# A circulant filter matrix from frequencies sorted by parity, and the latents' weights in two wider products

## The chip, the cores and the metric

The kernel runs on one core of one Trainium2 chip. The time is the device time of one execution in microseconds (us). Three runs of the kernel before gave a median of 418.75 us.

## The reference, cut to what matters

```python
D = _fractal_dimension(x)                 # from the first 1024 normalised values
filt = _wave_filter(D, E)                 # E = 256 complex factors, a function of |frequency|
x1 = ifft(fft(x, axis=-1) * filt, axis=-1).real
lat = x1 @ W_el + b_el                    # W_el: 256 x 24
bits = (sigmoid(lat) > 0.5)
corrected = _golay_correct(bits)
attn = x1 + corrected @ W_le + b_le
...
xn = _layernorm(x)
x = x + attn(xn) + ffn(xn)                # ffn: 256 -> 1024, exact gelu, -> 256, with biases
```

x has 2 x 4096 tokens of 256 float32 numbers. The filter depends only on the absolute frequency, so filtering is the product with a symmetric circulant matrix C of 256x256 whose first row c is a sum of cosines (and, by the way it is laid out here, of sines) with the filter as weights.

## The kernel before, in words

**Tiles.** The tokens are worked on in 16 chunks of 512, with the 256 features on two blocks of 128 partitions. In each chunk TensorE computes the hidden layer (`up`, L882, eight blocks m of 128 hidden units), its product with w2 (`down`, L900 and L905), the latents (`latents`, L926), the filter (`filtered`, L937), the code checks (`checks`, L950) and the correction's product (`le_products`, L956). Precision is kept with pairs: each float32 number is split into a "hi" part (rounded to the format float32r, which TensorE takes in one pass) and a "lo" part (the rest). ScalarE makes the gelu and the hi parts, VectorE the lo parts, the normalisation and the sums. GpSimd takes square roots and `uv`, the sums and differences of the two feature halves (`turn`).

**Sums and differences.** With u = first half + second half and v = first half - second half, the circulant falls apart into two 128x128 matrices, one for u and one for v. They are kept in `c_f` as two halves of 128 columns, and split into `c_hi` and `c_lo`. The latents' weights are the matrix's product with W_el, turned the same way.

**The work around the change** is in chunk 0, and is done once:
- SyncE's queue loads `basis` (L298) behind the weights; behind it stand `xt(1)`, `codes` and `latent`.
- VectorE makes `wel_t` from W_el (L817 to L819), then `bias` and `le_t` (L822, L823), for which ScalarE waits (L516).
- GpSimd computes `filt_w`, the 256 filter weights, two on each partition.
- ScalarE scales `basis` with them into `basis_w` (L526).
- TensorE makes the matrix in `p_l` (`circulant`, L1025), after `down(0, 4)`.
- ScalarE copies it to `c_f` and `c_hi` (L531, L532).
- TensorE multiplies `c_f` with `wel_t` in `p_g` (`latent_weights`, L1034 and L1035), after `down(0, 6)`.
- ScalarE casts that to `cw` (L536), waiting for `cw_made`; VectorE adds the low part (L837).
- Only then ScalarE makes the hi part of chunk 1's normalised columns (`columns_hi(1, 1)`, L411), and VectorE the lo part (`columns_lo`, L601), for which `up(1, 1, 0)` waits.

All orders are written out by hand: each engine runs its own list, and waits on semaphores. The products of `circulant` and `latent_weights` have plain float32 operands; in the trace each of them is two TensorE instructions of the same shape, with a weight load each. VectorE's list from the end of chunk 0 on:

```python
            scale(1, 1)
            hidden_lo(0, 7)
            ...
            columns_lo(1, 1)
            turned_lo(0)
            ...
            first_branch_chunk(1, 1)
```

and `first_branch_chunk` begins with the statistics (L569), `add_ffn` (L635), `hidden_lo(c, 0)` (L611), `aggregate` (L574) and `take_bits(b, ...)` (L616), for whose `word` TensorE waits before its second `latents`.

Of the kernel before, what the change touches and what calls it, by code (L numbers as in the profile page):

```python
# [7 lines left out]
F32, F32R, BF16, U32 = mybir.dt.float32, mybir.dt.float32r, mybir.dt.bfloat16, mybir.dt.uint32  # L8
ALU = mybir.AluOpType
# [3 lines left out]
P = 128  # L13
TOKENS, E, HID, LAT, SYN = 2 * 4096, 256, 1024, 24, 12
# [4 lines left out]
KB = E // P  # L19
MB = HID // P  # L20
HF = E // 2
# [12 lines left out]
SEG = 32  # L34
# [34 lines left out]
def build(nc, x, xt, small, latent, w1, w2, ident, consts, basis, codes, out):  # L69
    ctx = ExitStack()  # L70
    with ctx:
        def sb(name, shape, dt):
            return ctx.enter_context(nc.sbuf_tensor(name, shape, dt))

        def ps(name, shape, dt):
            return ctx.enter_context(nc.psum_tensor(name, shape, dt))

        def sem(name):
            return ctx.enter_context(nc.semaphore(name))
# [30 lines left out]
        con = sb("con", [P, K_END], F32)  # L110
        code_f = sb("code_f", [P, 2, P], F32)
        code = sb("code", [P, 2, P], BF16)
        bias = sb("bias", [P, KB], F32)
        wel_t = sb("wel_t", [P, 3, LAT], F32)
        basis_sb = sb("basis_sb", [P, KB, HF + E], F32)
        basis_w = sb("basis_w", [P, KB, E], F32)
        c_f = sb("c_f", [P, 2, HF], F32)
        c_hi = sb("c_hi", [P, 2, HF], F32R)
        c_lo = sb("c_lo", [P, 2, HF], F32R)
# [27 lines left out]
        filt_w = sb("filt_w", [P, KB], F32)  # L147
# [15 lines left out]
        p_l = ps("p_l", [P, BANK], F32)  # L163
        p_g = ps("p_g", [P, BANK], F32)
# [18 lines left out]
        basis_wd, c_made, c_copied, c_hi_ready = sem("basis_wd"), sem("c_made"), sem("c_copied"), sem("c_hi_ready")  # L183
        wel_turned, cw_made, cw_hi_ready, c_ready = sem("wel_turned"), sem("cw_made"), sem("cw_hi_ready"), sem("c_ready")
# [9 lines left out]
        turned, u_hi, u_lo = sem("turned"), sem("u_hi"), sem("u_lo")  # L194
# [22 lines left out]
        def half_tokens(part, g):  # L217

            return part[:, :, g * GTOK:(g + 1) * GTOK]

        def half_bank(g):

            return p_s[:, g, :].rearrange("p (k t) -> p k t", k=KB)
# [179 lines left out]
        def _(act):  # L403
# [23 lines left out]
            def gelu(c, m, first=False):  # L427

                act.wait_ge(up_done, MB * c + m + 1)
                if not (first and m < 2):  # L430

                    act.wait_ge(h_lo_done, MB * c + m - 1)
                nc.scalar.activation(h[m % 2][:], p_h[:, m % 2, :], ACT.Gelu,  # L433
                                     bias=small_sb[:, S_B1 + m:S_B1 + m + 1]).then_inc(gelu_done, 1)
# [74 lines left out]
            for g in range(2):  # L509
                last = nc.scalar.copy(half_tokens(xc0, g), half_bank(g))  # L510
# [12 lines left out]
            act.wait_ge(basis_in, 16)  # L523
            act.wait_ge(filt_made, 1)
            for k in range(KB):
                nc.scalar.mul(basis_w[:, k, :], basis_sb[:, k, HF:HF + E], filt_w[:, k:k + 1]).then_inc(basis_wd, 1)  # L526
            gelu(0, 7, first=True)
            hidden_hi(0, 7, first=True)
            act.wait_ge(c_made, 1)
# [22 lines left out]
        def _(dve):  # L552
# [6 lines left out]
            def then(ins):  # L559

                links[0] += 1
                ins.then_inc(link, 1)
                dve.wait_ge(link, links[0])
# [186 lines left out]
            for j in range(HALF):  # L750
                dve.wait_ge(x_first[j], 16)
                last = nc.vector.bn_stats(stats[:, j, :], x_sb[0][:, j, :])
# [4 lines left out]
            for j in range(HALF, CT):  # L757
                last = nc.vector.bn_stats(stats[:, j, :], x_sb[0][:, j, :])
# [55 lines left out]
            hidden_lo(0, 4)  # L814
            dve.wait_ge(small_in, 16)
            wel = small_sb[:, S_WEL:S_END].rearrange("p (k l) -> p k l", k=KB)
            nc.vector.tensor_tensor(wel_t[:, 0, :], wel[:, 0, :], wel[:, 1, :], ALU.add)  # L817
            nc.vector.tensor_tensor(wel_t[:, 1, :], wel[:, 0, :], wel[:, 1, :], ALU.subtract)
            nc.vector.tensor_tensor(wel_t[:, 2, :], wel[:, 1, :], wel[:, 0, :], ALU.subtract).then_inc(wel_turned, 1)  # L819
            then(nc.vector.tensor_tensor(bias[:], small_sb[:, S_BLE:S_BLE + KB], small_sb[:, S_B2:S_B2 + KB], ALU.add))  # L820
            dve.wait_ge(latent_in, 16)
            nc.vector.tensor_tensor(le_t[:, 0, :], latent_sb[:, 1:1 + HF], latent_sb[:, 1 + HF:1 + E], ALU.add)  # L822
# [31 lines left out]
        def _(pe):  # L854
            mm = nc.tensor.matmul
# [164 lines left out]

            def circulant():

                pe.wait_ge(basis_wd, KB)
                for k in range(KB):
                    last = mm(p_l[:, 0:E], basis_sb[:, k, 0:HF], basis_w[:, k, :], start=(k == 0), stop=(k == KB - 1))  # L1025
                last.then_inc(c_made, 1)

            def latent_weights():

                pe.wait_ge(c_copied, 1)  # L1030
                pe.wait_ge(wel_turned, 1)
                for k in range(KB):
                    at = SEG + k * LAT
                    mm(p_g[:, at:at + LAT], c_f[:, 0, :], wel_t[:, 0, :], start=True, stop=False, skip_group_check=True)  # L1034
                    last = mm(p_g[:, at:at + LAT], c_f[:, 1, :], wel_t[:, 1 + k, :], start=False, stop=True,  # L1035
                              skip_group_check=True)
                last.then_inc(cw_made, 1)

            def summed_over(at, n, parts, ready, done):
# [10 lines left out]
            for g in range(2):  # L1050

                pe.wait_ge(xn0_done, g + 1)
                for k in range(KB):
                    for j in range(HALF):
                        last = nc.tensor.transpose(half_bank(g)[:, k, j * P:(j + 1) * P],
                                                   xn0[:, g * HALF + j, k * P:(k + 1) * P], id_sb[:])
# [28 lines left out]
def constants():  # L1085

    import numpy as np

    f4 = np.float32
    con = np.zeros((P, K_END), f4)  # L1090
    lx = np.log(np.array(SCALES, np.float64))
    n = len(SCALES)
    den = n * np.sum(lx * lx) - np.sum(lx) ** 2

    coef = -(n * lx - np.sum(lx)) / den


    at = np.arange(FRE)
    row, half = 2 * (at // (2 * KB)) + at % 2, at // 2 % KB
    number = (E * row + P * half + np.arange(P)[:, None] + 1).reshape(P, 1, FRE)  # L1100
    con[:, K_MASK:K_MASK + NS * FRE] = (number <= np.array(PREFIX)[:, None]).reshape(P, NS * FRE)
    con[:, K_CLOG:K_CLOG + NS * FRE] = (np.log(number) * coef[:, None]).reshape(P, NS * FRE)
    con[:, K_NUM:K_NUM + FRE] = number[:, 0]
    con[:, K_INVN:K_INVN + NS] = [1.0 / n for n in PREFIX]

    r = np.arange(E)
    freq = np.where(r <= E // 2, r, r - E // 2)
    ang = 2.0 * np.pi * ((freq[:, None] * r[None, :]) % E) / E
    basis = np.where((r <= E // 2)[:, None], np.cos(ang), np.sin(ang)).astype(f4)
    ka = (freq / E).astype(f4) + f4(1e-8)  # L1110
    weight = np.where((r == 0) | (r == E // 2), 1.0, 2.0) / E / 2
    turned = np.concatenate([basis[:, :HF], basis[:, :HF] + basis[:, HF:], basis[:, :HF] - basis[:, HF:]], axis=1)
    by_block = lambda v: v.reshape(KB, P).T

    ka = ka.astype(np.float64)
    con[:, K_C1:K_C1 + KB] = by_block(np.pi - ka)
    con[:, K_C1 + KB:K_C1 + COLS] = by_block(np.pi / 2 + ka)
    con[:, K_C2:K_C2 + KB] = by_block(1.0 + 0.5 * ka)
    con[:, K_C2 + KB:K_C2 + COLS] = by_block(1.0 + 0.1 * ka * ka)
    con[:, K_ODD:K_ODD + PAIRS * COLS] = np.repeat(SINE[1::2], COLS)  # L1120
    con[:, K_EVEN:K_EVEN + PAIRS * COLS] = np.repeat(SINE[0::2], COLS)
    con[:, K_WK:K_WK + KB] = by_block(weight)
    con[:, K_WK + KB:K_WK + COLS] = 1.0
    a = np.array([[1, 1, 1, 0, 1, 1, 1, 0, 0, 0, 1, 1], [1, 1, 0, 1, 1, 1, 0, 0, 0, 1, 1, 0],
# [4 lines left out]
                  [1, 0, 0, 1, 1, 0, 0, 1, 1, 0, 0, 1], [0, 1, 1, 0, 0, 1, 1, 0, 0, 1, 1, 0]], np.int64)  # L1129
    rows = np.concatenate([a.T, np.eye(SYN, dtype=np.int64)], axis=1)  # L1130

    codes = np.zeros((P, 2, P), f4)
    fixed = np.zeros((P, GROUPS, SEG), f4)
    for par in range(2):
        here, before = SEG * par, SEG * (1 - par)
        codes[here:here + LAT, par, ROWS:ROWS + SYN] = rows.T
        fixed[:] = 0.0
        fixed[before:before + LAT, :, 0:LAT] = 25.0 * np.eye(LAT)[:, None, :]  # L1140
        fixed[2 * SEG, :, 0:LAT] = 9.5
        fixed[ROWS:ROWS + SYN, :, 0:SYN] = (1.0 - 13.0 * np.eye(SYN))[:, None, :]
        codes[:, par, 0:ROWS] = fixed.reshape(P, ROWS)
    return np.eye(P, dtype=f4), con, turned.astype(f4), codes.reshape(P, 2 * P)


def layouts(inputs):
# [37 lines left out]
```

## Time and profile before

| | us |
|---|---|
| median of three runs (lowest, highest) | 418.75 (418.73, 419.31) |
| the profiled execution, its own time | 418.89 |
| its span, first to last instruction | 417.1 |
| TensorE busy | 409.1 (98%) |
| VectorE busy | 307.3 (74%) |
| ScalarE busy | 218.7 (52%) |
| GpSimd busy | 73.7 (18%) |

How to read it: the profile shows one execution. PE is TensorE's products, PEld its weight loads (which overlap the products), DVE VectorE, ACT ScalarE, POOL GpSimd, SP SyncE. L1025 is line 1025 of the kernel before. The ends of products are modelled, so starts are safer than durations, and a stretch in which each product begins before the last has ended counts as busy. In rows of instructions the numbers are start, duration, engine, line, operation, output, inputs and their sizes; "x2" says that two neighbours were merged, and then the duration runs from the first one's start to the last one's end. A square bracket holds the engine's idle time before the row, and what ended it. The clock that TensorE was granted is 1.00 of full speed in all stretches shown.

### The profile page before, as it was taken

Reading aid. Unit: us, or ns where it says so; the run is one execution under the profiler, and the core shown is the slowest. Engines: PE = TensorE matmul, PEld = TensorE weight load, DVE = VectorE, ACT = ScalarE, POOL = GpSimd, SP = SyncE. Lnnn points to the kernel's source line nnn. Section 1 sums busy time; section 2 is a strip of 40 time slices with the busy share of each in tenths; the row PEclk is TensorE's granted clock in tenths of the full one; section 3 lists DMA queues with packets and bytes.
Section 4 is the critical chain, followed back from the end, with each engine's and each line's share of the span. In section 5 each row is a group of like instructions: output and inputs, shape, how many; then the busy total and the mean of one; then the engine's idle time right before and its main releaser. Section 6 shows DMA issues by size and latency. Waiting matters only on the chain.

```text
span 417.1 us, 5569 instructions
## 1 busy us (share of the span) xinstructions
PE 409.1 (98%) x1789; PEld 325.8 (78%) x1789; DVE 307.3 (74%) x503; ACT 218.7 (52%) x325; POOL 73.7 (18%) x102
## 2 busy tenths in 40 slices
PE   8998999999999999999999999999999999999996
PEld 4786787887888788787887878788787878878774
DVE  7888696968669686776867778686786868676654
ACT  3957446555365554536555464554536655464641
POOL 2161321212012121111212012121111212012000
PEclk9999999999999999999999999999999999999999
DMA  7562223133331123332122332223333111111011
GB/s 221 200 210 95 101 61 92 52 101 103 101 101 56 51 95 101 101 101 72 53 76 101 101 101 90 26 86 101 101 101 98 53 51 51 51 51 50 2 50 50
DMA packets 16495, 36.04 MB, mean 86 GB/s; under 512 B 5452, under 2 KB 8164, under 8 KB 16484
## 3 DMA queue, kind: packets, MB, share of 16 engines
q1 hardware_dynamic: 16340, 35.78, 27.2%
q10 hardware_dynamic: 144, 0.13, 0.1%
q8 instruction: 5, 0.08, 0.1%
q14 instruction: 6, 0.05, 0.1%
HBM read 27.45 MB, written 8.45 MB: 86 GB/s over the span
## 4 chain that ended last, share of the span: by engine, by line
PE 93%; DVE 4%; DMA 1%; issue 1%; ACT 0%; POOL 0%; SPq 0%; DVEq 0%
PE p_h L882 41%; PE p_f L900 27%; PE p_f L905 13%; PE p_s L937 5%; PE p_l L926 3%; PE p_s L956 2%; PE p_g L950 1%; DMA x_sb<-x 1%; DVE stats L569 1%; DVE xt_sb L644 0%; DVE xt_sb L650 0%; DVE xT_lo L601 0%; DVE w_lo L732 0%; DVE h_lo L611 0%; DVE xt_sb L726 0%
## 5 line engine op out<-in xcount | busy, mean ns | idle before, releaser
L433 ACT ACTIVATE h<-p_h,small_sb 128x512 f32<-128x512 f32 x128 | 88.1, 688 | 155.1 <-PE p_h L882 155.0
L611 DVE TENSOR_TENSOR h_lo<-h,h_hi 128x512 fp32r<-128x512 f32 x128 | 90.1, 704 | 71.4 <-ACT h_hi L441 71.2
L900 PE MATMUL p_f<-h_hi,w_hi 128*128 128x512 f32 x254 | 99.7, 392 | 0.0
L900 PE MATMUL p_f<-h_hi,w_lo 128*128 128x512 f32 x254 | 99.0, 390 | 0.0
L882 PE MATMUL p_h<-xT_hi,w_hi 128*128 128x512 f32 (+1 forms) x258 | 86.1, 415 | 1.5 <-DVE xT_lo L601 1.0
L441 ACT CAST h_hi<-h 128x512 fp32r<-128x512 f32 x128 | 79.4, 620 | 5.8
L882 PE MATMUL p_h<-xT_lo,w_hi 128*128 128x512 f32 (+1 forms) x258 | 79.6, 390 | 0.1
L882 PE MATMUL p_h<-xT_hi,w_lo 128*128 128x512 f32 (+1 forms) x258 | 79.5, 389 | 0.0
L905 PE MATMUL p_f<-h_lo,w_hi 128*128 128x512 f32 x254 | 78.2, 389 | 0.0
L363 POOL TENSOR_TENSOR uv<-xn 128x512 f32<-128x512 f32 x30 | 43.6, 1475 | 127.7 <-DVE xn L596 127.7
L882 PEld LDWEIGHTS p_h<-xT_hi,w_hi 128*128 128x128 f32 x258 | 48.3, 189 | 11.9 <-DVE xT_lo L601 1.5
L882 PEld LDWEIGHTS p_h<-xT_lo,w_hi 128*128 128x128 f32 x258 | 48.3, 188 | 10.8 <-DVE xT_lo L767 0.3
L882 PEld LDWEIGHTS p_h<-xT_hi,w_lo 128*128 128x128 f32 x258 | 48.3, 188 | 10.7
L900 PEld LDWEIGHTS p_f<-h_hi,w_hi 128*128 128x128 f32 x254 | 47.7, 188 | 10.3
L905 PEld LDWEIGHTS p_f<-h_lo,w_hi 128*128 128x128 f32 x254 | 47.7, 188 | 10.1
L900 PEld LDWEIGHTS p_f<-h_hi,w_lo 128*128 128x128 f32 x254 | 47.7, 188 | 10.0
L346 POOL TENSOR_TENSOR var_eps<-mv,eps 128x4 f32<-128x4 f32 (+1 forms) x17 | 3.9, 227 | 173.3 <-DVE mv L574 173.3
L601 DVE TENSOR_TENSOR xT_lo<-xn,xT_hi 128x1024 fp32r<-128x1024 f32 x15 | 32.7, 2179 | 0.8 <-ACT xT_hi L411 0.7
L635 DVE SCALAR_TENSOR_TENSOR xt_sb<-p_f,bias,xt_sb 128x512 f32 (+1 forms) x30 | 21.1, 746 | 12.5 <-PE p_f L905 12.5
L606 DVE TENSOR_TENSOR uv_lo<-uv,uv_hi 128x1024 fp32r<-128x1024 f32 x16 | 19.6, 1226 | 9.2 <-ACT uv_hi L418 9.2
L411 ACT CAST xT_hi<-xn 128x1024 fp32r<-128x1024 f32 x15 | 15.8, 1054 | 13.5 <-DVE xn L596 13.5
L591 DVE TENSOR_TENSOR xn<-xt_sb,rows_sb 128x1024 f32<-128x1024 f32 x15 | 18.3, 1223 | 5.9 <-DMA rows_sb<-rows_dram 5.5
(117 smaller groups left out, 331.4 us busy)
## 6 DMA issues: line engine op xcount, KB each, us to landing
xt_sb<-xt SPq DMA_DIRECT2D x16, 512.0 KB, 5.2
x_sb<-x SPq DMA_DIRECT2D x15, 512.0 KB, 4.5
rows_sb<-rows_dram SPq DMA_DIRECT2D x15, 512.0 KB, 4.1
out<-xt_sb SPq DMA_DIRECT2D x15, 512.0 KB, 2.9
xt_sb<-w SPq DMA_DIRECT2D x3, 512.0 KB, 7.3
xt_sb<-w SPq DMA_DIRECT2D x2, 256.0 KB, 4.1
basis_sb<-basis SPq DMA_DIRECT2D x1, 384.0 KB, 8.8
x_sb<-x SPq DMA_DIRECT2D x2, 128.0 KB, 2.1
```

The costliest lines, as they stand in the source:

```text
L363: nc.gpsimd.tensor_tensor(uv[:, k, :], columns[:, 0, :], columns[:, 1, :], op).then_inc(turned, 1)
L433: nc.scalar.activation(h[m % 2][:], p_h[:, m % 2, :], ACT.Gelu, bias=small_sb[:, S_B1 + m:S_B1 + m + 1]).then_inc(gelu_done, 1)
L441: nc.scalar.copy(h_hi[m % HR][:], h[m % 2][:]).then_inc(h_hi_done, 1)
L591: nc.vector.tensor_tensor(xn[:, :, :], columns(c), to_halves(rows_sb[par][:, 0, :]), ALU.subtract).then_inc(centred, 1)
L601: nc.vector.tensor_tensor(xT_lo[par][:, :, :], xn[:, :, :], xT_hi[par][:, :, :].bitcast(F32), ALU.subtract).then_inc(t_lo, 1)
L606: nc.vector.tensor_tensor(uv_lo[:, :, :], uv[:, :, :], uv_hi[:, :, :].bitcast(F32), ALU.subtract).then_inc(u_lo, 1)
L611: nc.vector.tensor_tensor(h_lo[m % HR][:], h[m % 2][:], h_hi[m % HR][:].bitcast(F32), ALU.subtract).then_inc(h_lo_done, 1)
L635: nc.vector.scalar_tensor_tensor(out=xc, in0=p_f[:, k, :], scalar=bias[:, k:k + 1], in1=xc, op0=ALU.add, op1=ALU.add).then_inc(ffn_added, 1)
L882: last = mm(p_h[:, m % 2, tok], w[:, k, m * P:(m + 1) * P], xp[par][:, k, tok], start=(n == 0), stop=(n == 3 * KB - 1))
L900: mm(p_f[:, a, :], w[:, m, a * HF:(a + 1) * HF], h_hi[r][:], start=(m == 0 and w is w2_hi), stop=False, skip_group_check=True)
L905: last = mm(p_f[:, a, :], w2_hi[:, m, a * HF:(a + 1) * HF], h_lo[r][:], start=False, stop=(m == MB - 1), skip_group_check=True)
L937: last = mm(p_s[:, k, :], w[:, k, :], xp[:, k, :], start=(n == 0), stop=False, skip_group_check=True)
```

## The change

The 256 frequencies are sorted: the even ones come first and make the first block of 128 rows of `basis`, the odd ones the second. A cosine or sine of an even frequency has the same value 128 columns on, one of an odd frequency the opposite value. So the matrix for the sums needs the even block alone, and the matrix for the differences the odd block alone. `circulant` was two accumulating products of 256 columns and is now two separate products of 128 columns; each waits only for its own half of `basis_w`. `basis` shrinks from 128x2x384 to 128x2x128 numbers, `basis_w` from 256 to 128 columns per block, and the weights of the frequencies are doubled on the host. `wel_t` is laid out for both feature halves side by side, so that `latent_weights` is two accumulating products of 48 columns instead of four of 24; the sum part is written twice, with a broadcast operand.

```diff
--- before.py
+++ after.py
@@ -111,9 +111,9 @@
         code_f = sb("code_f", [P, 2, P], F32)
         code = sb("code", [P, 2, P], BF16)
         bias = sb("bias", [P, KB], F32)
-        wel_t = sb("wel_t", [P, 3, LAT], F32)
-        basis_sb = sb("basis_sb", [P, KB, HF + E], F32)
-        basis_w = sb("basis_w", [P, KB, E], F32)
+        wel_t = sb("wel_t", [P, 2, KB, LAT], F32)
+        basis_sb = sb("basis_sb", [P, KB, HF], F32)
+        basis_w = sb("basis_w", [P, KB, HF], F32)
         c_f = sb("c_f", [P, 2, HF], F32)
         c_hi = sb("c_hi", [P, 2, HF], F32R)
         c_lo = sb("c_lo", [P, 2, HF], F32R)
@@ -523,7 +523,7 @@
             act.wait_ge(basis_in, 16)
             act.wait_ge(filt_made, 1)
             for k in range(KB):
-                nc.scalar.mul(basis_w[:, k, :], basis_sb[:, k, HF:HF + E], filt_w[:, k:k + 1]).then_inc(basis_wd, 1)
+                nc.scalar.mul(basis_w[:, k, :], basis_sb[:, k, :], filt_w[:, k:k + 1]).then_inc(basis_wd, 1)
             gelu(0, 7, first=True)
             hidden_hi(0, 7, first=True)
             act.wait_ge(c_made, 1)
@@ -814,9 +814,11 @@
             hidden_lo(0, 4)
             dve.wait_ge(small_in, 16)
             wel = small_sb[:, S_WEL:S_END].rearrange("p (k l) -> p k l", k=KB)
-            nc.vector.tensor_tensor(wel_t[:, 0, :], wel[:, 0, :], wel[:, 1, :], ALU.add)
-            nc.vector.tensor_tensor(wel_t[:, 1, :], wel[:, 0, :], wel[:, 1, :], ALU.subtract)
-            nc.vector.tensor_tensor(wel_t[:, 2, :], wel[:, 1, :], wel[:, 0, :], ALU.subtract).then_inc(wel_turned, 1)
+            other = wel[:, 1, :].unsqueeze(1).broadcast_to([P, KB, LAT])
+            nc.vector.tensor_tensor(wel_t[:, 0, :, :], wel[:, 0, :].unsqueeze(1).broadcast_to([P, KB, LAT]), other, ALU.add)
+            for k in range(KB):
+                last = nc.vector.tensor_tensor(wel_t[:, 1, k, :], wel[:, k, :], wel[:, 1 - k, :], ALU.subtract)
+            last.then_inc(wel_turned, 1)
             then(nc.vector.tensor_tensor(bias[:], small_sb[:, S_BLE:S_BLE + KB], small_sb[:, S_B2:S_B2 + KB], ALU.add))
             dve.wait_ge(latent_in, 16)
             nc.vector.tensor_tensor(le_t[:, 0, :], latent_sb[:, 1:1 + HF], latent_sb[:, 1 + HF:1 + E], ALU.add)
@@ -1020,20 +1022,20 @@
 
             def circulant():
 
-                pe.wait_ge(basis_wd, KB)
+
                 for k in range(KB):
-                    last = mm(p_l[:, 0:E], basis_sb[:, k, 0:HF], basis_w[:, k, :], start=(k == 0), stop=(k == KB - 1))
+                    pe.wait_ge(basis_wd, k + 1)
+                    last = mm(p_l[:, k * HF:(k + 1) * HF], basis_sb[:, k, :], basis_w[:, k, :], start=True, stop=True,
+                              skip_group_check=True)
                 last.then_inc(c_made, 1)
 
             def latent_weights():
 
                 pe.wait_ge(c_copied, 1)
                 pe.wait_ge(wel_turned, 1)
-                for k in range(KB):
-                    at = SEG + k * LAT
-                    mm(p_g[:, at:at + LAT], c_f[:, 0, :], wel_t[:, 0, :], start=True, stop=False, skip_group_check=True)
-                    last = mm(p_g[:, at:at + LAT], c_f[:, 1, :], wel_t[:, 1 + k, :], start=False, stop=True,
-                              skip_group_check=True)
+                for a in range(2):
+                    last = mm(p_g[:, SEG:SEG + KB * LAT], c_f[:, a, :], wel_t[:, a, :, :].rearrange("p k l -> p (k l)"),
+                              start=(a == 0), stop=(a == 1), skip_group_check=True)
                 last.then_inc(cw_made, 1)
 
             def summed_over(at, n, parts, ready, done):
@@ -1105,11 +1107,13 @@
 
     r = np.arange(E)
     freq = np.where(r <= E // 2, r, r - E // 2)
-    ang = 2.0 * np.pi * ((freq[:, None] * r[None, :]) % E) / E
+
+    r = np.argsort(freq % 2, kind="stable")
+    freq = freq[r]
+    ang = 2.0 * np.pi * ((freq[:, None] * np.arange(HF)[None, :]) % E) / E
     basis = np.where((r <= E // 2)[:, None], np.cos(ang), np.sin(ang)).astype(f4)
     ka = (freq / E).astype(f4) + f4(1e-8)
-    weight = np.where((r == 0) | (r == E // 2), 1.0, 2.0) / E / 2
-    turned = np.concatenate([basis[:, :HF], basis[:, :HF] + basis[:, HF:], basis[:, :HF] - basis[:, HF:]], axis=1)
+    weight = np.where((r == 0) | (r == E // 2), 1.0, 2.0) / E
     by_block = lambda v: v.reshape(KB, P).T
 
     ka = ka.astype(np.float64)
@@ -1141,7 +1145,7 @@
         fixed[2 * SEG, :, 0:LAT] = 9.5
         fixed[ROWS:ROWS + SYN, :, 0:SYN] = (1.0 - 13.0 * np.eye(SYN))[:, None, :]
         codes[:, par, 0:ROWS] = fixed.reshape(P, ROWS)
-    return np.eye(P, dtype=f4), con, turned.astype(f4), codes.reshape(P, 2 * P)
+    return np.eye(P, dtype=f4), con, basis, codes.reshape(P, 2 * P)
 
 
 def layouts(inputs):
```

## Rows read from the trace of the kernel before

**Rows 1.** The page, parts 1 and 4: TensorE's busy time, and the chain's shares by engine

```profile
PE 409.1 (98%) x1789; PEld 325.8 (78%) x1789; DVE 307.3 (74%) x503; ACT 218.7 (52%) x325; POOL 73.7 (18%) x102
...
PE 93%; DVE 4%; DMA 1%; issue 1%; ACT 0%; POOL 0%; SPq 0%; DVEq 0%
```

**Rows 2.** Windows, a later chunk: stretch, length, busy us (count) by engine, clock

```profile
59.89:84.80 24.91, 24.91 (x110) 20.05 (x110) 18.54 (x30) 13.06 (x19) 4.25 (x5) 1.00 0.35 105
```

**Rows 3.** Waits of TensorE, whole span: total us, times, longest (two of five)

```profile
PE p_h L882 <- DVE xT_lo L601: 1.0, 1, 1.0
...
PE p_l L926 <- DVE word L616: 0.5, 1, 0.5
```

**Rows 4.** Timeline, the first products of chunk 1

```profile
34.98 0.73 PE L882 MATMUL p_h<-xT_hi,w_hi 128*128 128x512 f32 x2 [1.02 <-DVE xT_lo L601]
```

**Rows 5.** The chain that ended last, 28 to 35 us: start, us, what

```profile
28.03 0.86 PE p_l L1025 x4
...
32.25 0.24 PE p_g L1035 x2
...
32.52 0.20 ACT cw L536
32.71 0.96 ACT xT_hi L411
...
33.70 1.23 DVE xT_lo L601
```

**Rows 6.** Timeline of VectorE

```profile
17.51 0.20 DVE L799 TENSOR_TENSOR fr_b<-con,fr_s 128x40 f32<-128x40 f32 x1
...
22.16 0.18 DVE L817 TENSOR_TENSOR wel_t<-small_sb 128x24 f32<-128x24 f32 x1
...
24.86 3.47 DVE L611 TENSOR_TENSOR h_lo<-h,h_hi 128x512 fp32r<-128x512 f32 x2 [1.70 <-ACT h_hi L441]
...
29.82 1.23 DVE L596 TENSOR_TENSOR xn<-xn,rows_sb 128x1024 f32<-128x1024 f32 x1
...
36.09 0.42 DVE L842 TENSOR_TENSOR le<-le_r,le_mid 24x256 bf16<-24x256 f32 x1
36.54 1.40 DVE L569 BATCH_NORM_STATS2 stats<-x_sb 128x6 f32<-128x256 f32 x4
```

**Rows 7.** Timeline of ScalarE in the second half of chunk 0

```profile
23.18 0.42 ACT L516 ACTIVATE le<-le_t 24x256 bf16<-24x256 f32 x1 [2.53 <-DVE le_t L823]
...
26.28 0.91 ACT L526 ACTIVATE basis_w<-basis_sb,filt_w 128x256 f32<-128x256 f32 x2
...
28.93 0.38 ACT L531 COPY c_f<-p_l 128x256 f32<-128x256 f32 x1 [0.52 <-PE p_l L1025]
...
32.52 0.20 ACT L536 CAST cw<-p_g 128x48 fp32r<-128x48 f32 x1 [2.93 <-PE p_g L1035]
```

**Rows 8.** Timeline of weight loads around the latents' products

```profile
31.62 0.30 PEld L1035 LDWEIGHTS p_g<-wel_t,c_f 128*128 128x128 f32 x2
...
32.29 0.19 PEld L900 LDWEIGHTS p_f<-h_hi,w_hi 128*128 128x128 f32 x1
```

**Rows 9.** Timeline of weight loads, 256-column products of the first chunk

```profile
9.12 0.31 PEld L882 LDWEIGHTS p_h<-xT_hi,w_hi 128*128 128x128 f32 x2
9.35 0.31 PEld L882 LDWEIGHTS p_h<-xT_hi,w_lo 128*128 128x128 f32 x2
```

**Rows 10.** Lines L1042 and L1035: duration ns least/median/most, starts, forms

```profile
L1042 PE MATMUL p_g<-fr_d,ones x2: 166/208/250, 19.4 to 19.5; 128*128 128x1 f32 x2
...
L1035 PE MATMUL p_g<-wel_t,c_f x4: 269/269/269, 31.6 to 32.2; 128*128 128x24 f32 x4
```

**Rows 11.** Timeline of SyncE: the issue of the load of basis

```profile
6.76 0.75 SPq L298 DMA_DIRECT2D basis_sb<-basis  x1
```

**Rows 12.** DMA issues: count, KB each, median us from issue to landing

```profile
basis_sb<-basis SPq DMA_DIRECT2D x1, 384.0 KB, 8.8
...
code_f<-codes SPq DMA_DIRECT2D x1, 128.0 KB, 9.0
```

## The prediction

> **What bounds the kernel now.** I read the page first. TensorE is busy for 409.1 of the 417.1 us, and the chain that ended last is TensorE for 93% [rows 1]. So there are two ways to gain: fewer TensorE instructions, or less of the time in which TensorE stands still. Next come the stretches of the trace. Each later chunk takes 24.91 us and TensorE is busy in all of it, with the granted clock at 1.00, which is the 2.4 GHz level, throughout [rows 2]. The waits of TensorE over the whole span are five, and the last two are those that matter here: 1.0 us for `xT_lo` and 0.5 us for `word` [rows 3]. Both lie between 34 and 41 us, behind the code that is changed, and none of the five lies after 42 us. So what is gained before chunk 1 starts is kept to the end, if chunk 1 really starts earlier.
>
> **Where the changed code lies.** It runs once, in chunk 0. `up(1, 1, 0)` starts at 34.98, and TensorE stood still for 1.02 us before it, from 33.96 [rows 4]. The chain shows why: the latents' products (L1034, L1035) until 32.49, ScalarE's cast of `cw` (L536), its cast `xT_hi` (L411), VectorE's `xT_lo` (L601), then TensorE [rows 5]. ScalarE works in order, so `columns_hi(1, 1)` stands behind the wait for `cw_made`, although its input `xn` was ready at 31.05 (L596 starts at 29.82 and takes 1.23) [rows 6]. ScalarE stood idle 2.93 us before L536 [rows 7]. After `xT_lo`, VectorE works without a gap (L606, L842, L569, L635, L611, L574, L616) until `word` (L569 starts 0.03 after L842 ended [rows 6]), and TensorE's second wait ends there [rows 3]. Both waits of TensorE therefore hang on the same event, the end of L1035, and move with it. This makes the changed products a critical stage, even though TensorE has an idle microsecond right behind them: shortening only other TensorE work behind `cw_made` would give nothing.
>
> **Products of the filter matrix.** Before, four instructions (two for each float32 product) of 256 columns follow each other; the chain has them from 28.03 and gives them 0.86 us, 0.215 each [rows 5]. After, there are again four, each with 128 columns. Half the streaming of 0.215 is 0.108. The weight load sets another floor. Near it are the loads of the 24-column products, which are so short that only loads pace them: from the second pair of loads to the first load behind the last pair, three pairs, it is 32.29 - 31.62 = 0.67 us, some 0.1125 per instruction [rows 8]. A row with about this amount of streaming is the 256-column single-pass product of the first chunk, whose pairs of loads are 0.23 apart, 0.115 each [rows 9]. I take 0.115: 4 x 0.115 = 0.46, a gain of 0.86 - 0.46 = 0.40 us. The bounds are 0 (the instructions keep the 0.215 of now) and 0.43 (pure streaming, 0.86 / 2). This gain reaches the latents' products, since TensorE works without a gap from one to the other and nothing it needs is late: `c_f` is copied at 29.31 [rows 7] and is wanted shortly before 31.62 [rows 8], or 0.40 earlier then; `h_lo` of m = 6 is ready when L611's pair ends at 28.33 [rows 6] and is wanted after 31.0.
>
> **The waits on `basis_wd`.** Before, one wait for both scaled halves, after, one for each. The two scalings end at 27.19 (26.28 + 0.91) [rows 7] and the chain comes to the products at 28.03 [rows 5], so neither wait binds: nothing. ScalarE's scalings shrink from 128x256 to 128x128. Halved at best, the stage of 0.91 falls to between 0.45 and 0.91. What is behind it, `gelu(0, 7)` and `hidden_hi(0, 7)`, is over 0.52 before ScalarE is released by `c_made` [rows 7]; the gain there is hidden, and since `c_made` comes only 0.40 earlier, no queue forms.
>
> **The latents' weights.** Four products of 24 columns become two of 48, eight instructions become four. A pair costs 0.67 / 3 = 0.223 between starts, so two pairs fewer are 0.45 us [rows 8]. The wider ones should take no more between starts, since even 128 streamed columns come to 0.108, under the pace of the loads. Their own duration grows, though: the longer of the two kinds is 250 ns at 1 column and 269 at 24, that is 19 ns for 23 columns [rows 10], so 24 more columns make the last one end 0.02 later. The gain is 0.43 us, with bounds of 0.40 (if the added columns were paid in all four) and 0.45.
>
> **VectorE.** The three `wel_t` operations of 128x24 take about 0.18 each [rows 6]. After, they are one of 128x48 with broadcast inputs and two of 128x24. The nearest row with a broadcast operand is L799, 128x40 in 0.20 [rows 6]. So 0.02 us more, between 0 and 0.05. They hold up `le_t`, for which ScalarE waits (2.53 us before L516 [rows 7]), and so `gelu(0, 5)` and then the whole gapless VectorE chain from L611 up to `xn`. But that chain delivers `xn` at 31.05, and ScalarE will want it at about 32.71 - 0.83 = 31.88, so 0.02 disappears in a cover of 0.8 us. With that cover gone it would cost its 0.02.
>
> **The transfer of `basis`** shrinks from 384 to 256 KB, in rows of 512 instead of 1536 bytes. It is issued at 6.76 [rows 11] and landed 8.8 us later [rows 12], at 15.6, and is wanted by L526 at 26.28 [rows 7]. Behind it in the queue are `xt(1)`, `codes` and `latent`; codes land 9.0 us after their issue [rows 12], some 17.5, and ScalarE wants them after L516, so after 23.18 [rows 7]. Either way nothing, with 5 us of cover.
>
> **Sum.** 0.40 + 0.43 = 0.83 us on the end of L1035. `xT_lo` then starts at 33.70 - 0.83 = 32.87 [rows 5]. TensorE finishes `down(0, 7)` at 33.96 - 0.83 = 33.13 and waits again, to 34.15. The profiled execution took 418.89 us, 1.79 more than its span (a constant part); less 0.83 that is 418.06. It lies 0.14 above the median of 418.75, so for the median I predict 418.75 - 0.83 = 417.92 us, a ratio of 0.9980.
>
> **A rule beside it.** The rows have the short instructions at 0.1125 to 0.115 each [rows 8, 9]. The Trainium skill, "TensorE: Matmul & The Clock Gate", section "Back-to-back issue gap", gives about 81 ns for each pair of load and product with 128 columns in a sustained stream, and "LDWEIGHTS (loading the stationary operand)" gives columns / 1.2, which is 107 ns for 128. By the 81 ns the filter matrix would gain 0.86 - 0.32 = 0.54 and the latents' weights only 4 x 0.081 - 0.02 = 0.30, together 0.84; the result would hardly differ. The rows speak for the load's 107 ns as the floor.
>
> **Rivals.**
> (A) The filter products keep their pace of 0.215, because float32 instructions are paced by something other than columns. For it: no float32 product of 128 columns that is not a transpose is in the trace. Against it: the 24-column ones run at 0.1125. Only 0.43 would be left: 418.32.
> (B) Another wait takes the place of `cw_made`, for instance VectorE in chunk 1 standing for something that doesn't move. `x(2)` is such a thing, but VectorE began L569 0.03 after L842 ended [rows 6], so there is no sign that it waited; `xn` would allow a move of up to 0.8 or more. Then nothing would be gained: 418.75.
> (C) Short instructions run quicker than the rows let me think (0.081 in the filter products, 0.1125 kept for the removed ones): 0.54 + 0.43 = 0.97: 417.78.
> (D) Slower. The broadcast `wel_t` operation is slow, as an input with a repeated stride might be. The VectorE chain from L611 at 24.86 to `xn` [rows 6] starts from ScalarE's wait for `le_t`. Delays up to about 0.83 + 0.83 = 1.7 us are covered or repaid by the gain; it decides from there, ten times the 0.18 of such an operation now. At 2.7 us it would be 419.75. Against it: L799 with its broadcast takes 0.20 [rows 6].
>
> **How the numbers follow.** What a measurement of this kernel can tell from no change is about 0.2%, 0.84 us; my forecast of 0.83 lies on that edge. Chances: the forecast, a gain of 0.75 to 0.90, 0.74; A 0.08; B 0.06; C 0.07; D and other losses 0.05. The forecast's case is split nearly in two by the edge, 0.36 above and 0.38 below. Faster: 0.36 + 0.07 = 0.43, and 0.02 for mixed cases, 0.45. Within: 0.38 + 0.08 + 0.06 less those 0.02, 0.50. Slower: 0.05. The likeliest case's own range is 417.85 to 418.0; the three runs shown scatter by 0.02 below and 0.56 above the median. The range that leaves out B and D and takes in A and C is 417.7 to 418.4.
>
> **What would show it.** Right: L1025's four instructions take about 0.46 us in the chain; the latents' products begin near 31.1 and are four; L536 starts near 31.69, L601 near 32.87, `up(1, 1, 0)` near 34.15; TensorE's waits are still 1.0 and 0.5 us; chunk 2 starts 0.83 earlier and every chunk still takes 24.91. Wrong: a start of L536 that moved by less than 0.75 (A), a start of chunk 2 that moved less than L536 did (B), `wel_t` operations above 0.3 us (D), or a new wait in the later chunks.

## The result, and the profile after

The changed kernel takes 415.85 us (median of 6 runs, 415.69 to 416.11), the kernel before in the same series 418.95: a ratio of 0.9927, 95% interval 0.9917 to 0.9936. That is 3.1 us less, where 0.83 were predicted, and it lies outside the range. The profiled execution's span fell from 417.1 to 414.1 us.

First the part that was predicted. The chain that ended last, of the kernel after, 28 to 35 us (start, us, what):

```profile
28.03 0.45 PE p_l L1028 x4
28.48 0.92 PE p_f L902 x4
...
31.21 0.39 PE p_g L1037 x4
...
31.63 0.20 ACT cw L536
31.83 0.96 ACT xT_hi L411
...
32.81 1.23 DVE xT_lo L601
```

Against [rows 5]: the filter products took 0.86 us and take 0.45, for the same four instructions. The latents' products took 0.82 (31.67 to 32.49) and take 0.39. The cast of `cw` moved from 32.52 to 31.63, `xT_lo` from 33.70 to 32.81. The timeline of TensorE at the start of chunk 1, after:

```profile
34.09 0.73 PE L884 MATMUL p_h<-xT_hi,w_hi 128*128 128x512 f32 x2 [1.04 <-DVE xT_lo L601]
```

It was at 34.98 [rows 4]: 0.89 us earlier, 0.83 was predicted. The waits of TensorE, after:

```profile
PE p_h L884 <- DVE xT_lo L601: 1.0, 1, 1.0
...
PE p_l L928 <- DVE word L616: 0.6, 1, 0.6
```

To within 0.1 us they are what they were [rows 3], and no new one stands behind them. So where are the other 2.1 us? Look at the chunks that the change doesn't touch. The chain of the kernel before, one later chunk (`latents`, `up`, `filtered`), and the start of the next chunk's `latents`:

```profile
88.42 0.93 PE p_l L926 x4
89.35 1.39 PE p_h L882 x6
90.74 1.40 PE p_s L937 x6
...
113.33 0.93 PE p_l L926 x4
```

The same of the kernel after:

```profile
87.35 0.91 PE p_l L928 x4
88.26 1.36 PE p_h L884 x6
89.62 1.36 PE p_s L939 x6
...
112.12 0.91 PE p_l L928 x4
```

From `latents` to `latents` it was 113.33 - 88.42 = 24.91 us and is 112.12 - 87.35 = 24.77. The products are the same in number, shape and order, there is no idle time in either, and the clock is 1.00 in both. Six products of 512 columns took 1.39 or 1.40 in this stretch, and now take 1.36. That is their pace in the rest of the chunk too, apart from a short stretch behind the 16-bit products of `checks` and `le_products`, which both kernels have (1.38). The start of TensorE's last product says it for the whole kernel. Before, then after:

```profile
412.59 0.39 PE L915 MATMUL p_f<-h_lo,w_hi 128*128 128x512 f32 x1
```

```profile
409.61 0.39 PE L917 MATMUL p_f<-h_lo,w_hi 128*128 128x512 f32 x1
```

From the start of chunk 1 it was 412.59 - 34.98 = 377.61 us and is 409.61 - 34.09 = 375.52, 2.09 less, which is 15 chunks by 0.14. With the 0.89 ahead of chunk 1 these are 2.98 of the span's 3.0 us.

### The profile page after: what moved, and what is told of

Same layout as the page of the kernel before. It is cut to its first block, busy times and chain, and to the rows that moved or that the text cites. A ratio compares the mean times of both kernels' runs of the same rounds, so it can differ in the third digit from the quotient of the medians.

```text
span 414.1 us, 5561 instructions
## 1 busy us (share of the span) xinstructions
PE 406.1 (98%) x1785; PEld 325.0 (78%) x1785; DVE 307.2 (74%) x503; ACT 218.7 (53%) x325; POOL 73.8 (18%) x102
## 4 chain that ended last, share of the span: by engine, by line
PE 93%; DVE 4%; DMA 1%; issue 1%; ACT 0%; POOL 0%; SPq 0%; DVEq 0%
PE p_h L884 41%; PE p_f L902 27%; PE p_f L907 14%; PE p_s L939 5%; PE p_l L928 3%; PE p_s L958 2%; PE p_g L952 1%; DMA x_sb<-x 1%; DVE stats L569 1%; DVE xt_sb L644 0%; DVE xt_sb L650 0%; DVE xT_lo L601 0%; DVE w_lo L732 0%; DVE h_lo L611 0%; DVE xt_sb L726 0%
```

## Experiments

**Where the tiles lie.** A product on TensorE has a stationary operand (the weights, loaded by an instruction of its own, PEld in the trace) and a moving one (the columns that are streamed past it). Both are tiles in SBUF, the on-chip memory. Tiles lie there in the order in which they are declared, each size rounded up to 32 bytes per partition. The change alters three sizes ahead of `c_f`, `c_hi`, `c_lo` and `cw`: `wel_t` 288 to 384 bytes, `basis_sb` 3072 to 1024, `basis_w` 2048 to 1024. So these four, and all tiles behind them, lie 2976 bytes lower. In the later chunks, `c_hi` and `c_lo` are the stationary operands of `filtered`, `cw` that of `latents`. The moving operands (`xT_hi`, `xT_lo`, `uv_hi`, `uv_lo`) and those of `up` and `down` are large tiles ahead of the altered ones and did not move.

**e1: the kernel before, with `wel_t` one slot larger.**

```diff
-        wel_t = sb("wel_t", [P, 3, LAT], F32)
+        wel_t = sb("wel_t", [P, 4, LAT], F32)
```

> The kernel before, with one line changed: wel_t is declared with 4 slots of 24 instead of 3, 384 bytes per partition instead of 288, and the fourth is not used. No instruction changes, but everything declared behind wel_t (basis_sb, basis_w, c_f, c_hi, c_lo, cw, idle, word, cor, le3 and others) moves by 96 bytes, so that the starts of these tiles, which are 32 past a multiple of 64 bytes in the kernel before, become multiples of 64, as in the changed kernel. Theory ALIGN (the 0.14 us that each later chunk gains come from where the tiles lie in SBUF): the chunks fall from 24.91 to 24.77 us, chunk 1 still starts at 34.98, and the time falls by 14 x 0.14 = 2.0 us, to about 416.8. Theory STREAM (they come from TensorE's program being shorter by four product and four load instructions, so that the loop's body lies elsewhere): nothing changes, 418.9. Theory HEAD (the later chunks gain because chunk 1 starts at another moment against the transfers): nothing changes, 418.9.

Measured: 417.01 us, ratio to before 0.9946 (0.9927 to 0.9966). The chain of e1:

```profile
88.29 0.91 PE p_l L926 x4
89.19 1.36 PE p_h L882 x6
90.55 1.36 PE p_s L937 x6
...
113.05 0.91 PE p_l L926 x4
```

113.05 - 88.29 = 24.76, and chunk 1 started at 35.04, as late as before. An unused fourth slot, without one instruction changed, brings the whole gain of the later chunks. STREAM and HEAD fall.

**e2: the changed kernel with a gap of 32 bytes.**

```diff
+        gap = sb("gap", [P, 8], F32)
         basis_sb = sb("basis_sb", [P, KB, HF], F32)
```

> The changed kernel with an unused tile of 32 bytes per partition declared ahead of basis_sb, so that the tiles behind it start 32 bytes past a multiple of 64 again, as in the kernel before. No instruction changes. ALIGN: chunks of 24.91 us again, and only the gain ahead of chunk 1 is left: 418.95 - 0.89 = 418.06 us. STREAM and HEAD: 415.85, as the changed kernel.

Measured: 417.52 us, ratio 0.9959 (0.9946 to 0.9972); chunks of 24.85, not the 24.91 that was expected. The place matters, but not as "a multiple of 64 or not".

**e3 and e4: which stationary operand.** Both are the kernel before with two gaps of 32 bytes.

```diff
 e3
+        gap = sb("gap", [P, 8], F32)
         cw = sb("cw", [P, KB, P], F32R)
+        gap2 = sb("gap2", [P, 8], F32)
         stats = sb("stats", [P, CT, 6], F32)
 e4
+        gap = sb("gap", [P, 8], F32)
         c_f = sb("c_f", [P, 2, HF], F32)
...
+        gap2 = sb("gap2", [P, 8], F32)
         cw = sb("cw", [P, KB, P], F32R)
```

> The kernel before with an unused tile of 32 bytes ahead of cw and another behind it: of the tiles behind wel_t, cw alone (the stationary operand of latents) starts at a multiple of 64 bytes, all others stay 32 past one. The slow stretch of the kernel before begins among the latents' products and runs on over the filter's products (c_hi, c_lo) and up(c, 2) and down(c, 0). ALIGN, if cw alone starts it and the filter's products inherit it: chunks of 24.77. ALIGN, if each misaligned stationary operand costs its own: between 24.77 and 24.91, nearer the upper end since six filter products stand against four of the latents. STREAM, HEAD, or tiles other than the stationary ones (word, cor, le3): 24.91.

> The counterpart: c_f, c_hi and c_lo start at multiples of 64 bytes, cw and everything behind it 32 past one. ALIGN, if cw alone starts the slow stretch: it is shorter, since the filter's products no longer feed it, or unchanged, 24.80 to 24.91. ALIGN, if the cost is the filter's: 24.77 to 24.80. STREAM, HEAD: 24.91.

Measured: e3 418.70 us and chunks of 24.88; e4 417.41 and 24.81 (one run each). In e3 only `cw` moved, and the later chunks gained 0.03; in e4 `c_hi` and `c_lo` moved too, and `filtered` takes 1.38 instead of 1.40 in the chain. So the place of each counts. How much of the 0.14 belongs to which these two don't say: as the table below shows, no operand reached in them the place where the cost is gone.

**e5 and e6: 64 bytes.** e6 is the changed kernel with a gap of 64 bytes ahead of `basis_sb`. e5 has two of 32, ahead of `id_sb` and ahead of `wel_t`.

```diff
 e5
+        gap = sb("gap", [P, 8], F32)
         id_sb = sb("id_sb", [P, P], F32)
...
+        gap2 = sb("gap2", [P, 8], F32)
         wel_t = sb("wel_t", [P, 2, KB, LAT], F32)
 e6
+        gap = sb("gap", [P, 16], F32)
         basis_sb = sb("basis_sb", [P, KB, HF], F32)
```

> The changed kernel with an unused tile of 32 bytes ahead of id_sb and another ahead of wel_t, so that id_sb, con, code_f and code also start at multiples of 64 bytes (they are 32 past one in both kernels), and wel_t and all behind it still do. In the changed kernel a slow stretch is left in every chunk, behind the check's product (L952), whose stationary operand is code. ALIGN: it shrinks or goes; it holds some 0.04 us of excess over the usual 0.227 per product, so 14 x 0.04 = up to 0.6 us less, 415.3 at best. If the stretch comes from the product being of 16-bit type and not from its place, nothing changes: 415.85.

> The changed kernel with an unused tile of 64 bytes ahead of basis_sb: all starts behind it are still multiples of 64, but no longer of 128. ALIGN with 64 bytes as the unit: chunks of 24.77 us, time 415.85. ALIGN with 128 or 256 bytes as the unit: chunks between 24.77 and 24.91.

Measured: e5 417.96 us (ratio 0.9972, 0.9962 to 0.9981), e6 418.01 (one run), with chunks of 24.90 and 24.89. ALIGN by 64 bytes falls: all the starts in question are multiples of 64 here, and the chunks are nearly as slow as before. The slow stretch behind the check's product didn't shrink in e5 either: the four products of `down` behind it still take 0.93.

**e7 and e8: the two parts of the change alone.** e7 is the kernel before with the new `wel_t` and the two wide products; e8 is the changed kernel with those undone.

```diff
 e7
-        wel_t = sb("wel_t", [P, 3, LAT], F32)
+        wel_t = sb("wel_t", [P, 2, KB, LAT], F32)
...
-                for k in range(KB):
-                    at = SEG + k * LAT
...
+                for a in range(2):
+                    last = mm(p_g[:, SEG:SEG + KB * LAT], c_f[:, a, :], wel_t[:, a, :, :].rearrange("p k l -> p (k l)"),
```

> The kernel before with the second part of the change alone: wel_t in the new layout of 384 bytes, and the latents' weights in two products of 48 columns. basis and the filter products stay. The new wel_t moves the tiles behind it by 96 bytes, as in e1. ALIGN: this part brings the whole gain of the later chunks, 2.0 us, and 0.45 of the gain ahead of chunk 1: about 416.5. STREAM or HEAD: 418.5.

> The changed kernel with the second part undone: wel_t in the old layout of 288 bytes and four products of 24 columns; the filter matrix from even and odd frequencies stays. The tiles behind wel_t start 32 past a multiple of 64 again. They lie a multiple of 1024 bytes below their place in the kernel before, where e2 had them 128 bytes elsewhere, and e2 lost 1.3 of the 2.1 us. ALIGN: the later chunks are slow again; if the place modulo 256 or more matters beside that modulo 64, 24.91 us each as before, and the time is 418.95 - 0.43 = 418.5; if only the place modulo 64 matters and e2's 24.85 belong to the changed program, 24.85 and 417.7. STREAM or HEAD: 24.77, 416.3.

Measured: e7 416.42 us (ratio 0.9934, 0.9919 to 0.9949), chunks of 24.77, chunk 1 at 34.50; e8 418.60 (ratio 0.9990, 0.9979 to 1.0001), chunks of 24.90. So the latents' part brings 0.66% of the 0.73% that both bring, most of it by the size of a tile. The filter part alone can't be told from no change, although its products take 0.45 us in its chain too. e8's tiles lie a multiple of 1024 bytes from their place before and cost the same as there, where e2's, 128 bytes from e8's, cost less.

**e9 to e12: which rule.** The gaps:

```diff
 e9   (the changed kernel)
+        gap = sb("gap", [P, 32], F32)
         basis_sb = sb("basis_sb", [P, KB, HF], F32)
 e10  (the changed kernel)
+        gap = sb("gap", [P, 8], F32)
         xt_sb = sb("xt_sb", [P, CHUNKS, KB, CTOK], F32)
 e11  (the changed kernel)
+        gap = sb("gap", [P, 40], F32)
         code = sb("code", [P, 2, P], BF16)
...
+        gap2 = sb("gap2", [P, 24], F32)
         wel_t = sb("wel_t", [P, 2, KB, LAT], F32)
...
+        gap3 = sb("gap3", [P, 32], F32)
         word = sb("word", [P, CTOK], BF16)
 e12  (the changed kernel)
+        gap = sb("gap", [P, 8], F32)
         xn = sb("xn", [P, KB, CTOK], F32)
...
+        gap2 = sb("gap2", [P, 56], F32)
         w1_hi = sb("w1_hi", [P, KB, HID], F32R)
```

> So far the later chunks take 24.77 us when c_hi, c_lo and cw start 128 past a multiple of 256 bytes, and 24.81 to 24.91 at 32, 64, 96, 160 and 192. All the large tiles (xT, uv, h, w1, w2) start 128 past a multiple of 256 too. Three theories are left. MULT: a stationary operand must start at a multiple of 128 bytes. SAME: TensorE runs undisturbed while successive stationary operands start at the same place modulo 256, and a change of that place costs a slow stretch behind it. PAIR: stationary and moving operand must start at the same place modulo 256. This kernel is the changed one with an unused tile of 128 bytes ahead of basis_sb, so that c_hi, c_lo and cw start at 0 modulo 256. MULT: chunks of 24.77. SAME and PAIR: slow, some 24.8 to 24.9.

> The changed kernel with an unused tile of 32 bytes ahead of xt_sb, the first tile, so that every tile moves by 32: large tiles, c_hi, c_lo and cw at 160 modulo 256, all alike. MULT: nearly all products are disturbed, well over 24.91 us for a chunk. SAME and PAIR: chunks of 24.77.

> The changed kernel with three unused tiles (160 bytes ahead of code, 96 ahead of wel_t, 128 ahead of word), so that code, le3, word and cor start 128 past a multiple of 256 as well, like all the rest of TensorE's operands in the later chunks. The slow stretches that the changed kernel still has behind the check's product (about 0.045 us of excess) and behind the correction's (0.014) go by SAME and PAIR: chunks of about 24.71, 14 x 0.06 = 0.8 us less, 415.0. If these stretches come from the 16-bit type, or by MULT (le3, word and cor were at 0 before): 24.77 for the correction's part, at best code's gone: 415.2 to 415.85.

> The changed kernel with an unused tile of 32 bytes ahead of xn and one of 224 ahead of w1_hi: the moving operands xT, uv, h_hi and h_lo start at 160 modulo 256, the stationary ones (w1, w2, c_hi, c_lo, cw) stay at 128. SAME and MULT: chunks of 24.77. PAIR: all products disturbed, over 24.91.

Measured: e9 417.16 us, chunks of 24.86; e10 416.14, 24.77; e12 425.56, 25.40 (one run each); e11 415.89 (ratio 0.9926, 0.9913 to 0.9940), 24.77. The chain of e12, in which only the moving operands were shifted:

```profile
88.93 0.93 PE p_l L930 x4
89.87 1.40 PE p_h L886 x6
91.27 1.40 PE p_s L941 x6
...
107.33 1.40 PE p_h L886 x6
...
114.33 0.93 PE p_l L930 x4
```

Here `up`'s products are slow to the end of the chunk (1.40 at 107.33), where the other kernels have 1.36 again. And the chain of e10, in which stationary and moving operands were shifted together:

```profile
87.56 0.91 PE p_l L929 x4
88.47 1.36 PE p_h L885 x6
89.83 1.36 PE p_s L940 x6
...
112.33 0.91 PE p_l L929 x4
```

MULT falls by e10 (xT, uv, h, w1, w2, c_hi, c_lo and cw at 160 modulo 256, which is no multiple of 128, and as fast as after) and by e9 (c_hi, c_lo and cw at a multiple of 128, and slow). SAME falls by e12 (all stationary operands alike, and everything slow). PAIR foretold all three. That 256 is the unit, and not 128 or 512, shows in e9 (128 apart, slow) and e11: there `c_hi`, `c_lo` and `cw` lie 256 bytes further from the moving tiles, modulo 512, than in the changed kernel, and the chunk takes the same 24.77. The table has the start of the stationary operand less that of the moving one, modulo 256 bytes, from the compiled programs, and a chunk's length, taken from `latents` to `latents` in the chain:

| kernel | `c_hi`, `c_lo` | `cw` | chunk, us |
|---|---|---|---|
| after, e1, e7, e10, e11 | 0 | 0 | 24.76 to 24.77 |
| e4 | 192 | 224 | 24.81 |
| e2 | 32 | 32 | 24.85 |
| e9 | 128 | 128 | 24.86 |
| e3 | 160 | 192 | 24.88 |
| e5, e6 | 64 | 64 | 24.89 to 24.90 |
| before, e8 | 160 | 160 | 24.90 to 24.91 |
| e12 (w1, w2 too) | 224 | 224 | 25.40 |

e11 also answers its own question: with `code`, `le3`, `word` and `cor` at one place with the rest, nothing more is gained (24.77). What makes the stretch behind the check's product slow stays open.

**A rival that no run was made for.** PAIR speaks of a product's own two operands. The traces let another pair stand: a stationary operand and the moving operand of the product ahead, which still streams while the weights are loaded. In the changed kernel the load of `cw` starts at 86.97, about when the second of the two products of `up` in the first row starts (0.23 behind 86.74), and 0.22 before the first product of `latents` at 87.19. From the timelines of TensorE and of its weight loads, after:

```profile
86.74 0.61 PE L884 MATMUL p_h<-xT_lo,w_hi 128*128 128x512 f32 x2
86.97 0.41 PEld L928 LDWEIGHTS p_l<-xT_hi,cw 128*128 128x128 f32 x2
```

In the later chunks both readings foretell the same, since all moving tiles lie alike there. Chunk 0 has a place where they differ: `basis_sb` and `basis_w`, the operands of `circulant`, match each other in every kernel, but in some they don't match the operands of `down` on either side. e8, where they are 160 apart from those:

```profile
28.18 0.45 PE p_l L1026 x4
28.63 0.93 PE p_f L900 x4
29.56 0.46 PE p_f L905 x2
30.02 0.93 PE p_f L900 x4
30.94 0.46 PE p_f L905 x2
31.41 0.13 PE p_g L1036 x2
```

The ten products of `down` from 28.63 to 30.94 take 2.31 here. In the kernels with the narrow filter products they take 2.28 when `basis_sb` and `basis_w` lie 0 apart from the tiles of `down` (after, e10, e11), and also at 32 (e2), 2.29 at 128 (e9), 2.30 at 64 (e5, e6) and 2.31 at 160. With the wide ones they take 2.31 or 2.32 in every kernel. Were a product's own operands all that counts, those behind the narrow ones would be equal. The differences are 0.01 to 0.03 us in one trace each, so this is a hint and not a test. Shown is that the costs are gone when all these operands lie at one place modulo 256; which two of them have to agree is not.

## Why the prediction was wrong

- **The step that failed** is the sum as a list of what chunk 0 does. Of the changed code the prediction said "It runs once, in chunk 0", and it expected that "every chunk still takes 24.91". But three declarations were changed too, and they set where `c_hi`, `c_lo` and `cw` lie, which the later chunks read. This term was left out, and it is the largest: 2.09 us. No rival held it either.
- **The filter products:** 0.86 to 0.45, a gain of 0.41 against 0.40. Four instructions with 128 float32 columns take 0.112 each. The row paced by weight loads was the right one to take: the pace is the same with 24, 48 and 128 columns. Rival A is refuted.
- **The latents' weights:** 0.82 to 0.39, 0.43 as predicted. With 48 columns instead of 24 the instructions keep their spacing, and the longer kind takes 275 ns at most against 269 [rows 10]: 0.01 more, not 0.02. By the instructions' pace of 0.11 (four in a row here, and four in `circulant`), rival C's 0.081 is refuted. The Trainium skill, "TensorE: Matmul & The Clock Gate", section "Back-to-back issue gap", gives about 81 ns for 128 columns in a sustained stream; the trace does not agree for these float32 products, with 0.112 each. The products begin at 31.21; by the prediction's own sum it was 31.67 - 0.40 = 31.27, and not the 31.1 that it names as a sign.
- **What lies between them:** the twelve products of `down` from 28.90 to 31.67 took 2.77 us and take 2.73 (28.48 to 31.21). This 0.04 makes up most of the difference between 0.89 and 0.83, and the prediction had no term for it. Neither part of the change brings it alone: e7, with the place of the changed kernel and wide filter products, has 2.77 here, e8, with narrow ones and the old place, 2.78.
- **Carried to the end:** right. ScalarE and VectorE moved by the same 0.89, both waits of TensorE kept their length to within 0.1, and rival B didn't come. The start of chunk 1 itself scatters by some 0.2 us between executions: 34.94 to 35.16 in before, e1, e3 and e4, whose chunk 0 has the same instructions, and 34.08 to 34.39 in after, e2, e5, e6, e9, e10 and e11. The terms above are therefore taken from within the chain.
- **VectorE and the transfer:** the wide `wel_t` operation took 0.20 us as L799 does, `le_t` was ready 0.09 later, and it was hidden. `basis` landed 9.1 us after its issue instead of 8.8 [rows 12], hidden as well. It shrank to 128 KB, as the page after shows, and not to the 256 that the prediction has; with 10 us of cover this changed nothing. Rival D is refuted.
- **The chances** were spread around the edge of 0.2% by a sum thought good to 0.1 us. The scatter of the terms was priced, a term not in the list was not.

## What to carry to other kernels

Read a diff for its declarations too: a size changed anywhere moves every tile declared behind it, and in a kernel bound by TensorE that can be worth more than the instructions. Compare the pace of untouched products in the two traces first: here 1.39 against 1.36 us for six found the cause. With a repeated stage it is cheap to let all stationary and moving operands of its float32r products start at one place modulo 256 bytes, by padding the declarations, and to keep such padding explicit, so that the next edit doesn't undo it.

## What the runs showed of the hardware

TensorE's single-pass float32r products with 128 stationary and 512 moving columns follow each other every 0.227 us (1.36 for six) when stationary and moving operands all start at the same place modulo 256 bytes in SBUF, be it 128 (after) or 160 (e10). With the starts 224 apart it is 0.233 (1.40 for six, e12), all through the chunk, 25.40 us instead of 24.77. When only ten of a chunk's products are so placed, the products behind them are slow for a while too: before, `up` behind `latents` took 1.39 though its own operands match. The cost is no simple function of the distance (the table: 128 costs less than 64 or 160), and what in the chip makes it so is not shown by these runs, nor whether a product's stationary operand has to agree with its own moving operand or with that of the product ahead. Nor do they show the same for operands of other types or sizes.
